# Attention and a mixture-of-experts layer: one program body for all slot widths on VectorE and ScalarE, and an earlier load of a slot's first w2 tiles

## The reference, cut to what matters

```python
router_probs = softmax(x_flat @ gate_w)                 # 4096 tokens, 8 experts
topk_w, topk_idx = top_k(router_probs, 2)               # weights of the two are normalised
h = silu(ragged_dot(x_sorted, w1)) * ragged_dot(x_sorted, w3)   # 1024 -> 3584
out_sort = ragged_dot(h, w2)                            # 3584 -> 1024
out = sum over k of topk_w * out_sort                   # back in the order of the tokens
```

## Time and profile before

| | us |
|---|---|
| median of 3 runs | 7752.39 (7752.11 to 7757.93) |
| profiled execution, its own time | 7751.41 |
| its span, first to last instruction | 7749.7 |

### The profile page before, as it was taken

One profiled execution on the slowest core, in us unless ns is written; L12 is line 12 of the kernel. 1 busy time (PEld: TensorE's weight loads), 2 busy tenths in 40 slices (PEclk: granted clock), 3 DMA queues, 4 the chain that ended last, 5 costly groups with the idle time before them and its releaser, 6 DMA issues.

```text
span 7749.7 us, 139241 instructions
## 1 busy us (share of the span) xinstructions
PE 7408.1 (96%) x45405; PEld 6571.4 (85%) x45406; DVE 5043.2 (65%) x8017; ACT 2858.9 (37%) x4875; POOL 922.9 (12%) x1344
## 2 busy tenths in 40 slices
PE   8968999999999999999999999999999999999998
PEld 4547877788779999888779999978778999999998
DVE  6767766677656665577656665567766666566655
ACT  2323334333443334333343334433343333433343
POOL 2330010100111000100101001100101001010111
PEclk9979999999999999999999999999999999999999
DMA  3333446544664446544564445544465445644465
GB/s 118 108 103 134 158 161 197 168 159 159 196 185 143 144 148 195 161 159 159 182 192 156 143 153 188 176 151 157 172 193 162 152 149 180 190 135 147 145 195 159
DMA packets 683875, 1246.39 MB, mean 161 GB/s; under 512 B 50528, under 2 KB 286448, under 8 KB 683632
## 3 DMA queue, kind: packets, MB, share of 16 engines
q1 hardware_dynamic: 584240, 935.24, 37.1%
q0 software_dynamic: 99392, 309.05, 12.1%
HBM read 840.81 MB, written 405.38 MB: 161 GB/s over the span
## 4 chain that ended last, share of the span: by engine, by line
PE 88%; issue 2%; DVE 2%; POOL 0%; ACT 0%; DMA 0%; DVEq 0%; POOLq 0%; ACTq 0%
PE pair L1695 57%; PE pair L1728 29%; PE pair L1816 1%; DVE wl L1335 1%; PE pair L1797 0%; DVE sil L1338 0%; POOL out_x L1933 0%; DVE sil L1556 0%; DMA xg<-in_L_ffn_w 0%; DVE sil L1335 0%; DVE xl L1335 0%; DVE hid L1338 0%; ACT wh L1108 0%; DMA part<-x_rows,id_g 0%; DVE sums L1335 0%
## 5 line engine op out<-in xcount | busy, mean ns | idle before, releaser
L1695 PE MATMUL pair<-xh,wh 128*128 128x264 f32 (+2 forms) x9408 | 2520.4, 322 | 71.3 <-ACT part L1108 21.2
L1695 PE MATMUL pair<-xh,wl 128*128 128x264 f32 (+2 forms) x9408 | 2538.1, 324 | 0.0
L1695 PE MATMUL pair<-xl,wh 128*128 128x264 f32 (+2 forms) x9408 | 2528.8, 323 | 0.0
L1335 DVE TENSOR_TENSOR wl<-raw,wh 128x512 fp32r<-128x512 f32 (+2 forms) x1875 | 1260.9, 693 | 925.5 <-ACT wh L1108 923.9
L1695 PEld LDWEIGHTS pair<-xh,wh 128*128 128x128 f32 x9408 | 1581.7, 190 | 227.6 <-issue 86.7
L1695 PEld LDWEIGHTS pair<-xh,wl 128*128 128x128 f32 x9408 | 1573.7, 189 | 138.0
L1695 PEld LDWEIGHTS pair<-xl,wh 128*128 128x128 f32 x9408 | 1570.5, 189 | 138.1
L1108 ACT ACTIVATE wh<-raw 128x512 fp32r<-128x512 f32 (+2 forms) x1875 | 1135.1, 628 | 1329.9 <-PE pair L1728 627.2
L1728 PE MATMUL pair<-wh,wl 128*128 128x264 f32 (+2 forms) x4704 | 1257.8, 322 | 0.0
L1728 PE MATMUL pair<-wl,wh 128*128 128x264 f32 (+2 forms) x4704 | 1255.5, 321 | 0.0
L1728 PE MATMUL pair<-wh 128*128 128x264 f32 (+2 forms) x4704 | 1143.6, 326 | 63.2 <-DVE wl L1335 42.9
(11 more groups left out here) (253 smaller groups left out, 5486.3 us busy)
## 6 DMA issues: line engine op xcount, KB each, us to landing
raw<-in_L_ffn_w SPq DMA_DIRECT2D x226, 1024.0 KB
raw<-hd SPq DMA_DIRECT2D x720, 272.0 KB
hd<-hid SPq DMA_DIRECT2D x112, 1088.0 KB, 4.4
hd<-sil SPq DMA_DIRECT2D x112, 816.0 KB, 6.8
raw<-w2s SPq DMA_DIRECT2D x256, 256.0 KB
w2v<-in_L_ffn_w POOLq DMA_DIRECT2D x112, 512.0 KB, 3.6
xg<-in_L_ffn_w POOLq DMA_DIRECT2D x112, 512.0 KB, 4.3
w2s<-w2v POOLq DMA_DIRECT2D x112, 512.0 KB, 5.2
```

The lines of the kernel that those rows point to most:

```text
L1335: return V.tensor_tensor(out, a, b, ALU.subtract)
L1695: mm = pe.matmul(to[:, c, 0:hi - lo], entry(w, e)[:, ks], x[:, e, k, lo:hi], start=begin and k == 0 and i == 0, stop=k == KH - 1 and i == ...
```

## The change

In VectorE's and ScalarE's programs one slot body takes the place of three. Each operation that reads or writes PSUM by chunks, or that is followed by such an operation on the same data, is put into a function of the number of columns and stands twice, once for 544 and once for 512 columns, behind a branch on the width (`by_banks`). The splits of the hidden values and three of the four silus always take 544 columns. A slot of 528 columns is handled as 544 on these two engines, and TensorE cuts its chunks at 272 + 256 instead of 264 + 264. In VectorE's c22 for a = 0, the wait for v stands behind the first `down_sum` now.

In GpSimd's program the load of a pair of w2 tiles is a function of its own. The first pair of the next slot is loaded in front of the fourth scatter of the old one, with the waits for the splits and the turned rows of the whole old slot; the pairs after it are loaded behind the store of the pair before.

```diff
+            def by_banks(width, body):       # ScalarE; VectorE has the same with dve
+                with act.If(width > BANK // 8):
+                    body(COLS)
+                with act.Else():
+                    body(BANK)
...
-            def unit(s, i, a, cols, after):
+            def unit(s, i, a, width, after):                 # ScalarE
...
+                by_banks(width, first_sum)
                 for e in range(EP):
                     if e == 3 and a == 0:
+                        by_banks(width, first_silu)
...
-                silu(sil[:, 3, 0:cols], sil[:, 3, 0:cols]).then_inc(s_sil, 1)
+                silu(sil[:, 3, 0:COLS], sil[:, 3, 0:COLS]).then_inc(s_sil, 1)
...
-                copy(down_h(wh, par)[:, 0:cols], rawh[b][:, 0:cols]).then_inc(s_hhi, 1)
+                copy(down_h(wh, par), rawh[b]).then_inc(s_hhi, 1)
...
                 with act.If(width > 0):
-                    with act.If(width > BANK // 8):
-                        with act.If(width > WIDTHS[-2] // 8):
-                            slot(s, WIDTHS[-1])
-                        with act.Else():
-                            slot(s, WIDTHS[-2])
-                        act.nop()
-                    with act.Else():
-                        slot(s, BANK)
-                    act.nop()
+                    slot(s, width)
+                act.nop()
...
+                def v_sum(cols):                             # VectorE
+                    product_done(s, i, a, 4)
+                    plus(in_sbuf(v, cols), in_sbuf(s1, cols), in_psum(b2, cols)).then_inc(s_v, 1)
+                def c22(cols):
+                    dve.wait_ge(s_v, g + 2)
+                    plus(in_sbuf(to[:, 3], cols), in_sbuf(v, cols), in_psum(b4, cols)).then_inc(s_c22, 1)
...
+                by_banks(width, u2_sum)
+                following(3)
+                after(2)
+                if a == 1:
+                    by_banks(width, h11)
+                after(3)
+                by_banks(width, v_sum)
+                if a == 0:
+                    dve.wait_ge(s_sst, pr * 16 + 16)
+                    down_sum(s, i, 0)
+                by_banks(width, c22)
+                after(4)
+                if a == 0:
+                    down_sum(s, i, 1)
+                else:
+                    by_banks(width, h22)
+                by_banks(width, c12)
+                after(5)
+                if a == 0:
+                    down_sum(s, i, 2)
+                else:
+                    by_banks(width, first_t)
+                by_banks(width, c21)
                 after(6)
                 if a == 0:
                     down_sum(s, i, 3)
                 else:
+                    by_banks(width, last_t)
...
-                return [(0, 0, n)] if n <= BANK else [(0, 0, n // 2), (1, n // 2, n)]
+                return [(0, 0, n)] if n <= BANK else [(0, 0, COLS // 2), (1, COLS // 2, n)]
...
+            def load_first_pair(s, e, ticked):               # GpSimd
+                pool.wait_ge(s_w2lo, s * STEPS + 2)
+                pool.wait_ge(s_hlo, s * STEPS + 2)
+                pool.wait_ge(s_xt, s * 16 + 16)
+                load_pair(e, 0, ticked)
...
                 with pool.Fori(0, PAIRS - 1) as i:
-                    stage_pair(s, e, i, s * TICKS + i * 2 + 4)
+                    store_sums(s, i, s * TICKS + i * 2 + 5)
+                    load_pair(e, i + 1, s * TICKS + i * 2 + 6)
...
-                for k in range(1, 4):
-                    scatter(s, k, width, ticked + 9 + k)
+                for k in range(1, 3):
+                    scatter(s, k, width, ticked + 8 + k)
+                load_first_pair(s + 1, slot_value(pool, 0, s + 1, E - 1), ticked + 11)
+                scatter(s, 3, width, ticked + 12)
                 pool.wait_ge(s_sc, s * 320 + 320)
...
+            load_first_pair(0, slot_value(pool, 0, 0, E - 1), 4)
             with pool.Fori(0, SLOTS) as s:
```

More of the change, by code:

```diff
@@ L1191, in results_out @@
                         copy(in_sbuf(other[d], cols), in_psum(pair[d], cols)).then_inc(s_acc[d], 1)
+                if p == 0:
+                    by_banks(width, first)
+                elif p == 5:
+                    by_banks(width, sixth)
             def scaled_rows(s, p):
@@ L1270, in down_phase @@
                         step((p + 1) * PAIRS)
-                        results_out(s, p, cols)
+                        results_out(s, p, width)
                         step((p + 1) * PAIRS + 1)
@@ L1299, in begin_down @@
                     elif e in (3, 4):
-                        h_hi(s, e - 3, cols)
-                unit(s, i, 1, cols, begin_down)
-                down_phase(s, cols)
+                        h_hi(s, e - 3)
+                unit(s, i, 1, width, begin_down)
+                down_phase(s, width)
             act.wait_ge(s_clear, 1)
@@ L1338, in plus, with by_banks @@
                 return V.tensor_tensor(out, a, b, ALU.add)
+            def by_banks(width, body):
+                with dve.If(width > BANK // 8):
+                    body(COLS)
+                with dve.Else():
+                    body(BANK)
             def weight_sum(s, i, a, n, fresh=False):
@@ L1415, in down_sum, with unit @@
                     less(a12, a12, a11).then_inc(s_w2sum, 1)
-            def unit(s, i, a, cols, after, following):
+            def unit(s, i, a, width, after, following):
                 g = s * UNITS2 + i * 2 + a
@@ L1546, in scaled_rows, with merge, sums_of @@
+                by_banks(width, evict)
+            def merge(s, width):
+                def sums_of(cols):
+                    for d in range(4):
+                        dve.wait_ge(s_acc[d], s * EVENTS + 1 + 2 * 5 + 2)
+                        plus(whole[d][:, 0:cols], whole[d][:, 0:cols], other[d][:, 0:cols]).then_inc(s_xv, 1)
+                by_banks(width, sums_of)
+            def scaled_rows(s, p, width):
                 k = OUTS[p]
                 nh = HALVES_OUT[k][1]
-                dve.wait_ge(s_wt, s + 1)
@@ L1549, in scaled_rows @@
-                if cols > BANK:
+                with dve.If(width > BANK // 8):
+                    dve.wait_ge(s_wt, s + 1)
                     dve.wait_ge(s_tlo, s * EP + (EP if k == 0 else 2 * EP))
@@ L1666, in _ @@
                 with dve.If(width > 0):
[L1667 to L1675 removed]
+                    slot(s, width)
+                dve.nop()
         @block.tensor
```

238 lines of the change are left out of this document (107 added, 131 removed).

## The result

The changed kernel takes 7675.05 us (median of 4 runs, 7667.01 to 7680.66) beside 7752.25 for the kernel before in the same comparison (4 runs, 7750.94 to 7757.93): ratio 0.9898, interval 0.9886 to 0.9911. The forecast was 7688, which is a ratio of 0.9917. Faster was right; the gain is about 79 us by the ratio, not 64.5. The profiled execution took 7680.66 us with a span of 7679.2, against 7749.7 before.

The account below looks back on a forecast made before the run. TensorE, busy 96% of the span, was taken as the bound. Slot changes give -65.25 + 0.7 = -64.5 us, all other terms 0: 7751.4 to 7686.9 profiled, median 7688, range 7675 to 7718.

Parts of the forecast that it names:

- What bounds the kernel, and the excess: TensorE bounds; first units of seven slots after a slot change take 65.25 us more than middle units.
- One body: At slot changes, fewer jumps between bodies let VectorE and ScalarE start sooner; TensorE's waits for s1 and u2 go.
- The pattern: Change into the 544 slot, taken as model for all: VectorE's first operation 5.35 us after TensorE's first matmul.
- The first w2 pair: Load issued before the last scatter is ready at about 1455, so the first down_sum no longer waits.
- neither half pays much alone: At slot changes, merged bodies with the late load still lose 6.4 us each; early load alone removes only c22 waits.
- What is late next: After the change c22 ends at 16.0 us, product 6 begins at 16.7; first units become normal, net -64.5 us.
- Branches in the middle, 0: Width branches on VectorE and ScalarE within a slot cost TensorE 0; upper end 22 us.
- 544 columns, 0: VectorE and ScalarE handling 544 columns instead of 512 or 528: splits take 720 ns instead of 690, cost 0.
- 272 + 256 for 264 + 264: TensorE's new cut of 528 slots leaves a couple of matmuls at 246.6 ns: 0, bounds -16 to +21 us.
- rival D: The cut at 272 in 528 slots costs +21 or -16 us: 7709 or 7672; chance 9%.
- The sum: 7751.4 - 64.5 = 7686.9 us for the profiled execution, predicted median 7688.
- Rival E: VectorE's pair loop, grown to about 175 instructions, no longer stays resident: +341 us, about 8093; chance 5%.

Follow-up runs that it names:

- e12: Changed kernel with the first w2 pair's load behind the last scatter's issues, still ahead of the wait for its landing; 7681.50 us, ratio 0.9909.
- e3: Changed kernel with GpSimd's old program, the first w2 load behind all scatters' landing; 7738.59 us, ratio 0.9974.
- e2: Changed kernel with TensorE's 528 slots cut at 264 + 264 again; 7699.73 us, ratio 0.9926.
- e9: Changed kernel with 600 never-executed memsets at the head of VectorE's pair loop, jumped over each turn; 8578.58 us, ratio 1.1071.
- e10: Changed kernel with 200 never-executed memsets at the head of VectorE's pair loop, jumped over each turn; 8578.38 us, ratio 1.1070.
- e5: Kernel before (three bodies, late load) with only the cut changed to 272 + 256, 528 slots using the 544 body; 7744.98 us, ratio 0.9982.
- e6: Changed kernel with 264 + 264 columns in 528 slots, the second chunk beginning at column 272; 7670.72 us, ratio 0.9886.
- e1: Changed kernel unaltered, run again to show its scatter; 7685.51 us, ratio 0.9910.
- e7: Changed kernel with 600 nops meant to lengthen VectorE's loop, none compiled in, so the changed kernel once more; 7688.01 us, ratio 0.9907.
- e8: Changed kernel with 272 + 256 columns in 528 slots, the second chunk beginning at column 264; 7689.23 us, ratio 0.9909.

## Why the prediction was right or wrong

- **What bounds the kernel, and the excess.** Right. 65.25 us were to be had, and 65.42 went from the first units, some 0.7 of it by the cut.
- **One body.** Right. The pattern held: VectorE's idle "issue" is 3.34 to 4.03 us at the seven changes, forecast 3 to 4; ScalarE's 1.37 to 1.43, forecast under 2. TensorE waits for neither u2 nor s1: at the first change u2 ends 9.5 us into the slot, forecast 9.1, and product 4 begins at 11.2.
- **The first w2 pair.** Right, and early enough by a wide margin: e12 issues it 19 us later and VectorE waits 1.45 us. The time was right too. It has to be counted from the slot's first matmul, since the two executions lie 8 us apart there: the forecast had the data ready at 1455, 4.4 us before 1459.36, and they landed at 1462.6, 5.0 us before 1467.61. And "neither half pays much alone" was right, but its price for the late load (6.4 us at each change) was too low: e3's first units lose (196.64 - 141.57) / 7 = 7.9, because the wait is counted from a VectorE that now arrives sooner.
- **What is late next.** Right: nothing. e2, without the cut's term, has a gain of 64.7 us at the slot changes in its windows, for the forecast 64.5.
- **Branches in the middle, 0.** Right: units 2 to 28 take 526.45 and 568.14 us in both kernels, and c22's margin grew from 0.22 to 0.69 us, forecast 0 to 0.3 more. The rule of the Trainium skill weighed there ("Runtime: NRT & Kernel Launch", "Instruction fetch mechanics", on stalls at taken far branches) shows its weight at the far jumps, those between the bodies before and those in e9 and e10, and none on the short branches here.
- **544 columns, 0.** Right, by the same windows.
- **"272 + 256 for 264 + 264", taken as 0. This is the step that failed.** It is worth -14 us (e5 alone; e2 undone 14.2), -15.1 by the matmul intervals of the profile: -23.8 up and +8.7 down. I had a line through lengths, bounds of -16 to +21 (1.6 x 10584 makes -17), and chose the middle "since 256 lies next to the two points of the line". That line has only lengths on it. 123.3 ns at 264 columns was not a point of a slope: e6 runs the same 264 columns in 121.1. It carried a surcharge for the place of the second chunk, which the new cut removes. The second fault is that one row of the up phase priced all 21168 matmuls; in the down phase the new cut costs time instead. So that the total came near my lower bound, the 7672 of rival D, is luck: neither bound had the place or the phase in it, and the lower one was drawn from the point at 264 (drawn from the line's own end at 272, the slope of 0.446 puts 256 columns at 118.2 ns and the term at -34 us). The row could have warned: from 264 to 272 columns 123.3 and 125.3 ns give 0.25 ns a column, from 272 to 512 it is 0.446. It also shows the weight loads busy for all of a unit at 544 and 528 and for 15.68 of 19.51 us at 512, so the points need not stand under one limit; no run tested that.
- **The sum.** -64.5 - 14 to -15 makes -79 to -80, and the first comparison's ratio gives -79. That they agree to 1 us is luck: the same kernel gained 70 us in e1's comparison and 71 in e7's, where its medians, 7685.51 and 7688.01, lie at the forecast of 7688, and e2, without the cut, gained 56. What is firm is the difference of 14 us between kernels of one comparison, twice, and the windows. They settle that the cut has a term of its own; what in the chip makes 264 dear is not settled.
- **Rival E, 5%.** It did not happen, but the reason given was weak. "Against it: the attention's loop executes 273 instructions" is true and didn't show where the limit lies, which e10 puts under about 390 for a loop with a long jump in it. The size is open: e10 loses 10.4 us in a turn and lies 829 us above the kernel before, where the forecast had 5.2 us and +341, but most of that is the jump over 200 instructions, which rival E did not have. The jump back takes 2.74 us there, which the 3.0 us of slack would hide by the prediction's own reckoning. The 3.0 us were about right: 10.37 us of idle time became a TensorE wait of 7.01. The Trainium skill's two lines of 256 instructions ("Advanced Engine Details and Errata", "ISA Cache") let 175 fit wherever they start. A loop of about 390 fits them only if it starts early enough in a line, and no trace shows where it starts, so e10 neither bears this rule out nor contradicts it.

## What to carry to other kernels

When two delays lie one behind the other at the same place, price the edits together: alone they gave 10 and 16 us in the windows (3 and 8 in the totals), together 65. A matmul's cost is not a function of its column count alone: compare chunks at the same start column before drawing a line through lengths, and try the start column as a knob of its own; here the old lengths with the second chunk moved to 272 were the fastest of five. A price read in one phase need not hold in another. Before merging bodies in a loop, count its instructions, and measure a padded copy: here about 190 were free, and about 390 with a jump over 200 of them cost 8 us of TensorE's time in every turn.

## What was not expected of the hardware

- Start column of the moving operand: a second chunk of 264 columns at 264 costs 123.3 ns a matmul, at 272 121.1.
- In the down phase 272 + 256 columns cost 124.9 to 125.6 ns a matmul, 264 + 264 124.0 to 124.7, over all kernels here.
- The same code in slots of the same width of one execution runs at 121.11 or 121.94 ns a matmul, steady for all of the slot (549.24 or 553.01 us); e2, e6, e8 and e12 show one value each in their three slots. Not explained.
- VectorE's loop with a forward jump over 200 instructions: 2.74 us at the jump back and 7.62 at the forward jump right behind it, but 2.93 at the same forward jump in the first turn; with 600 instructions jumped over 2.76, 7.64 and 2.93. The changed kernel's jump back takes 0.23 us.
- The attention and routing part in front of the first slot varies: it ends at 602.06 us in the profile of the kernel before and at 604.1 to 612.4 in the others.
